# A new order and new bank numbers for the steps of a software-pipelined Trainium2 kernel

## The reference

```python
x = L0_attn_a_hidden_states                                  # (16, 256, 128)
x = x + _L0_attn_a_ref(_layernorm(x, axis=-1), ...)          # gated log-linear attention, 32 heads of 64
x = x + _L0_ffn_ref(_layernorm(x, axis=-1), ...)             # "layer 0"
x = x + _L0_attn_b_ref(_layernorm(x, axis=-1), ...)          # gated mix of 9 shifted copies
x = x + _L0_ffn_ref(_layernorm(x, axis=-1), ...)             # "layer 1", same weights
```

## Time and profile before

| | |
|---|---|
| time, three runs | 2206.03, 2209.48, 2211.31 us (median 2209.48) |
| the profiled execution | 2206.03 us, its span from first to last instruction 2204.2 us |
| mean granted TensorE clock | 0.963 of full speed |
| busy share of the span | PE 89%, PEld 68%, DVE 79%, ACT 67%, POOL 42% |
| chain that ended last | PE 66%, DVE 17%, ACT 6%, issue 5%, POOL 4%, DMA 1% |

### The profile page before, as it was taken

One profiled execution on the slowest core, in us unless ns is written; L12 is line 12 of the kernel. 1 busy time (PEld: TensorE's weight loads), 2 busy tenths in 40 slices (PEclk: granted clock), 3 DMA queues, 4 the chain that ended last, 5 costly groups with the idle time before them and its releaser, 6 DMA issues.

```text
span 2204.2 us, 48465 instructions
## 1 busy us (share of the span) xinstructions
PE 1965.1 (89%) x16928; PEld 1494.5 (68%) x16928; DVE 1738.6 (79%) x4399; ACT 1486.3 (67%) x3143; POOL 929.0 (42%) x1299
## 2 busy tenths in 40 slices
PE   4779888999999999999999999999999999996756
PEld 2556666686767677776767777676767777674534
DVE  6666787989888888889898888989888888754543
ACT  3646667868676777868686877868676877744323
POOL 5212362625444453635445453635445453523221
PEclk9889999999999999999999999999999999998868
DMA  5020221130312122130312222130212222121010
GB/s 155 7 56 11 50 57 50 36 60 21 60 44 57 52 57 53 33 60 22 57 48 57 52 57 53 33 61 21 58 48 57 52 54 53 34 53 46 13 46 6
DMA packets 202306, 104.59 MB, mean 47 GB/s; under 512 B 126664, under 2 KB 188240, under 8 KB 196944
## 3 DMA queue, kind: packets, MB, share of 16 engines
q1 hardware_dynamic: 202064, 101.48, 20.2%
HBM read 67.60 MB, written 33.55 MB: 46 GB/s over the span
## 4 chain that ended last, share of the span: by engine, by line
PE 66%; DVE 17%; ACT 6%; issue 5%; POOL 4%; DMA 1%; SPq 0%; DVEq 0%; POOLq 0%; ACTq 0%
PE psB L861 8%; PE psA L711 6%; PE psA L686 5%; PE psA L849 5%; PE psB L849 4%; PE psA L617 4%; PE psA L790 3%; DVE work L1201 3%; DVE nmax L1276 3%; PE psB L617 2%; PE psB L790 2%; PE psA L678 2%; PE psB L775 2%; PE psA L861 2%; ACT att L980 2%
## 5 line engine op out<-in xcount | busy, mean ns | idle before, releaser
L1228 DVE TENSOR_TENSOR att<-att,QK 128x1024 f32<-128x1024 f32 x192 | 267.6, 1427 | 19.1 <-ACT att L980 17.6
L1201 DVE SCALAR_TENSOR_TENSOR work<-psA,c_conv_w,work 128x254 f32<-128x254 f32 (+1 forms) x540 | 231.2, 472 | 23.8 <-ACT work L943 23.8
L1515 POOL TENSOR_TENSOR own<-X,ccoef 128x512 f32<-128x512 f32 x128 | 169.4, 1328 | 147.5 <-PE psA L686 68.9
L861 PE MATMUL psB<-c_w,hid 128*128 128x128 f32 x1664 | 221.7, 280 | 1.5 <-DVE hid L1349 0.7
L1412 POOL TENSOR_SCALAR var_eps<-lnmv 128x2 f32<-128x2 f32 x128 | 40.7, 318 | 430.9 <-DVE lnmv L1087 429.4
L861 PEld LDWEIGHTS psB<-c_w,hid 128*128 128x128 f32 x1664 | 211.2, 196 | 10.8 <-issue 1.5
L617 PE MATMUL psA<-xnT_a,c_w_in 128*128 128x256 f32 x640 | 189.3, 401 | 19.7 <-DVE hid L1201 11.3
L1276 DVE TENSOR_REDUCE nmax<-psB 128x2 f32<-128x512 f32 x256 | 168.6, 680 | 47.3 <-PE psB L752 47.3
L1357 DVE SCALAR_TENSOR_TENSOR ff<-psB,w_e,ff 128x128 f32<-128x128 f32 x416 | 126.5, 346 | 83.4 <-PE psB L861 81.4
L1026 ACT ACTIVATE pt<-psB 128x512 f32<-128x512 f32 x304 | 176.5, 633 | 11.7 <-PE psB L776 11.7
L1049 ACT ACTIVATE hid<-psB,c_b 128x256 f32<-128x256 f32 x233 | 105.5, 477 | 101.5 <-PE psB L849 99.9
...
## 6 DMA issues: line engine op xcount, KB each, us to landing
qk_scr<-qparts SPq DMA_DIRECT2D x128, 192.0 KB, 2.5
...
q_max<-qk_scr SPq DMA_DIRECT2D x256, 32.0 KB, 1.9
k_max<-qk_scr SPq DMA_DIRECT2D x256, 32.0 KB, 1.8
...
low<-lvl_scr SPq DMA_DIRECT2D x256, 1.5 KB
...
```

Source lines behind the costliest of these rows:

```text
L861: m = e.matmul(t[:, i * P:(i + 1) * P], hb[:, j, i * P:(i + 1) * P], w_2[:, 2 * k + j, :], start=(j == 0), stop=(j == 1))
L1201: m = e.scalar_tensor_tensor(out=cv[:, back:], in0=t[:, 0:T - back], scalar=conv_w[:, c, tap:tap + 1], in1=cv[:, back:], op0=ALU.mult, op1 ...
L1228: e.tensor_tensor(att[:, :, :], att[:, :, :], bc(QK[:, kq, :], 1, HG), ALU.mult).then_inc(att_done, 1)
L1515: e.tensor_tensor(own_b[k % 2][:, :].rearrange("p (h c) -> p h c", c=HD), X[:, tt, h0 * HD:(h0 + HG) * HD].rearrange("p (h c) -> p h c", c ...
```

## The change

`PERIOD` is replaced as a whole. It still holds the same 303 hops, each once; no instruction is added, taken out or resized by the text itself, and `order()`, `build()` and everything else stay. What is new is the order, the lags that belong to another cut of the turn, and most bank digits. The number of table loads follows from the order.

```diff
 PERIOD = """
-... zact0.6+1 xcopy0.4+1 zgate0.1+1@52 smax0.1+2@3576 zact0.1+1 silu0.6+1
-zgate0.3+1@04 rowmax0.0+2 silu0.7+1 zact0.3+1 mix1.1+3@14 tail1.4+4@5 rowmax0.1+2 coef0.0+1 mix1.2+3@1 mix1.3+3@7
-mix1.4+3@6 mix1.5+3@0 tail1.5+4@3 tail1.6+4 mix1.6+3@5 place0.0+1@7 relu1.0+4 mix1.7+3@2 mix1.8+3@3 taps0.8+1 lvl0.7+1
-tap0.8+1 rowmax0.2+2 own0.0+1 mix1.9+3@6 up1.0+4@05 conv0.8+1@01 mix1.10+3@5 zact0.7+1 zgate0.7+1@65 smax0.2+2@0732
-rowmax0.3+2 wexp0.0+1 weigh0.0+1@54 weigh0.1+1@10 xt0.6+1@7 weigh0.2+1@45 wexp0.1+1 wexp0.2+1 smax0.3+2@3216
-zgate0.4+1@40 mix1.11+3@3 xcopy0.6+1 zact0.4+1 prod0.0+1 ...
...
+... place0.0+1@1 ... xt0.4+1@0 zact0.6+1 zgate0.5+1@24 rowmax0.0+2
+smax0.0+2@0563 zgate0.6+1@72 zgate0.2+1@17 zact0.2+1 zact0.1+1 smax0.1+2@5126 zgate0.1+1@73 mix1.1+3@47 tail1.4+4@5
+rowmax0.1+2 coef0.0+1 mix1.2+3@3 mix1.3+3@2 mix1.4+3@3 tail1.5+4@4 tail1.6+4 up1.0+4@25 mix1.5+3@6 mix1.6+3@3
+up1.1+4@40 conv0.8+1@17 taps0.8+1 tap0.8+1 zgate0.7+1@63 own0.0+1 relu1.1+4 relu1.0+4 mix1.7+3@4 zact0.7+1 xt0.6+1@0
+mix1.8+3@2 smax0.2+2@1365 rowmax0.2+2 xcopy0.6+1 silu0.8+1 experts1.0+4@4 mix1.9+3@2 mix1.10+3@0 weigh0.0+1@40
+rowmax0.3+2 weigh0.2+1@12 wexp0.0+1 smax0.3+2@3765 wexp0.2+1 experts1.1+4@4 down1.0+4@3 v0.0+2@1 mix1.11+3@0 relu1.2+4
+up1.2+4@27 lvl0.6+1 weigh0.1+1@04 acc1.0+4 wexp0.1+1 down1.1+4@5 weigh0.3+1@63 wexp0.3+1 zgate0.4+1@70 prod0.0+1
+mix1.12+3 xt0.7+1@1 ... maxt0.0+2@3 ... gates0.1+0@6 xcopy0.7+1 ... xcopy0.5+1
...
```

More of the change, by code:

```diff
@@ L123 @@
 PERIOD = """
[L124 to L128, removed]
@@ L144 @@
-maxt0.0+2@7 xt0.7+1@5 gated0.0+1 fn1.0+3 xt0.5+1@0 gates0.1+0@6 xcopy0.5+1 acc1.1+4 up1.3+4@27 prod0.1+1 own0.1+1
-xcopy0.7+1 relu1.3+4 gates0.2+0@63 sum0.1+1@1 fn1.1+3@2 prod0.2+1 gated0.1+1 exps0.0+2 own0.2+1 es0.0+2@6304 own0.3+1
-q1.0+3@7 own0.4+1 sum0.2+1@2 gates0.3+0 weigh0.4+1@1674 ep0.0+2@0 wexp0.4+1 exps0.1+2 gated0.2+1 es0.1+2@3167
-ocopy0.0+2 down1.2+4@5 q1.1+3@4 gates0.4+0@3 ep0.1+2@1 es0.2+2@5634 ocopy0.1+2 acc1.2+4 up1.4+4@12 sum0.3+1@0
-weigh0.5+1@6715 prod0.3+1 prod0.4+1 gated0.3+1 ep0.2+2@4 es0.3+2@2630 gates0.5+0 exps0.2+2 sum0.4+1@7 weigh0.6+1@1432
@@ L149 @@
-ep0.3+2@6 sum0.5+1@0 own0.5+1 relu1.4+4 weigh0.7+1@4521 prod0.5+1 own0.6+1 wexp0.5+1 exps0.3+2 ocopy0.2+2 prod0.6+1
-wexp0.6+1 gated0.5+1 acc1.3+4 down1.3+4@6 tail0.0+2@45 ocopy0.3+2 prod0.7+1 wexp0.7+1 sum0.6+1@3 tail0.1+2@1
-sum0.7+1@0 gated0.6+1 gated0.4+1 gated0.7+1 own0.7+1 tail0.2+2@4 up1.5+4@51 down1.4+4@3 relu1.5+4 smax1.0+3@4751
-outp0.0+1@2 ssq0.0+1@6 gates0.6+0 smax1.1+3@4350 ssq0.1+1 acc1.4+4 ssq0.2+1 ssq0.3+1 smax1.2+3@1437 outp0.1+1
-smax1.3+3@4305 tail0.3+2
+weigh0.6+2@2610 gated0.4+2 exps0.3+3 tail0.0+3@53 sum0.5+2@2 ocopy0.2+3 load_x0.0+0 ocopy0.3+3 relu1.5+5 prod0.6+2
@@ new lines @@
+wexp0.6+2 tail0.1+3@7 weigh0.7+2@1463 v1.0+4@0 prod0.7+2 own0.7+2 acc1.4+5 tail0.2+3@5 down1.4+5@7 down1.5+5@4
+sum0.6+2@1 wexp0.7+2 acc1.5+5 smax1.0+4@0574 lvl0.0+1 sum0.7+2@6 smax1.1+4@1503 outp0.0+2@2 gated0.5+2 smax1.2+4@4560
+ssq0.0+2@3 lvl0.1+1 ssq0.1+2 gated0.6+2 rowmax1.0+4 gated0.7+2 ssq0.2+2 ssq0.3+2 smax1.3+4@1574 up1.6+5@60 rowmax1.1+4
+relu1.6+5 tail0.3+3 rowmax1.2+4 outp0.1+2 tail0.4+3@0 up1.7+5@74 rowmax1.3+4 maxt1.0+4@1 relu1.7+5 conv0.0+1@56
+lvl0.2+1 outp0.2+2 tap0.0+1 tail0.5+3@0 fn0.0+2 lvl0.3+1 down1.6+5@3 acc1.6+5 relu0.1+3 up0.1+3@24 taps0.0+1
@@ new lines @@
+es1.0+4@1032 exps1.0+4 up0.0+3@71 relu0.0+3 lvl0.4+1 exps1.1+4 tail0.6+3 ep1.0+4@0 es1.1+4@3514 acc1.7+5 down1.7+5@7
+conv0.1+1@26 tap0.1+1 ocopy1.0+4 experts0.0+3@3 ep1.1+4@5 experts1.2+5 es1.2+4@7134 exps1.2+4 fn0.1+2@0 taps0.1+1
+experts0.1+3@7 ocopy1.1+4 ocopy1.2+4 ep1.2+4@1 q0.0+2@4 experts1.3+5 es1.3+4@0257 exps1.3+4 gates0.0+0 down0.0+3@1
+conv0.2+1@20 tap0.2+1 up0.2+3@36 down0.1+3@5 relu0.2+3 up0.3+3@41 silu0.0+1 silu0.1+1 tap0.3+1 conv0.3+1@67 acc0.0+3
+taps0.2+1 bcp0.0+1 down0.2+3@3 relu0.3+3 xt0.0+1@5 q0.1+2@0 up0.4+3@24 acc0.1+3 acc0.2+3 relu0.4+3 silu0.2+1
@@ new lines @@
+rowmax0.3+2 weigh0.2+1@12 wexp0.0+1 smax0.3+2@3765 wexp0.2+1 experts1.1+4@4 down1.0+4@3 v0.0+2@1 mix1.11+3@0 relu1.2+4
+up1.2+4@27 lvl0.6+1 weigh0.1+1@04 acc1.0+4 wexp0.1+1 down1.1+4@5 weigh0.3+1@63 wexp0.3+1 zgate0.4+1@70 prod0.0+1
+mix1.12+3 xt0.7+1@1 lvl0.7+1 sum0.0+1@2 zact0.4+1 maxt0.0+2@3 acc1.1+4 gates0.1+0@6 xcopy0.7+1 prod0.1+1 xcopy0.5+1
+xt0.5+1@4 fn1.0+3 prod0.2+1 up1.3+4@03 relu1.3+4 own0.1+1 gated0.0+1 gates0.2+0@57 down1.2+4@1 own0.2+1 exps0.0+2
+acc1.2+4 es0.0+2@3627 sum0.1+1@4 fn1.1+3@0 prod0.3+1 sum0.2+1@5 gates0.3+0 own0.3+1 weigh0.4+1@2716 gated0.1+1
@@ L154 @@
+wexp0.4+1 ep0.0+2@3 q1.0+3@0 ocopy0.0+2 up1.4+4@72 own0.4+1 es0.1+2@4105 gated0.2+1 own0.5+1 exps0.1+2 sum0.3+1@6
+gates0.4+0@4 relu1.4+4 gated0.3+1 ep0.1+2@1 ocopy0.1+2 q1.1+3@5 prod0.4+1 es0.2+2@4236 gates0.5+0 exps0.2+2
+down1.3+4@0 acc1.3+4 prod0.5+1 gates0.6+0 weigh0.5+1@1745 own0.6+1 ep0.2+2@3 es0.3+2@2671 sum0.4+1@4 ep0.3+2@7
+wexp0.5+1 up1.5+4@53
 """
```

17 lines of the change are left out of this document (6 added, 11 removed).

## The result

| | before | after |
|---|---|---|
| time | 2210.39 us median of four (2206.03 to 2212.87) | 2223.94 us median of four (2221.42 to 2225.14) |
| ratio | | 1.0062, 95% interval 1.0043 to 1.0081 |
| span of the profiled execution | 2204.2 us | 2222.1 us |
| mean granted TensorE clock | 0.963 | 0.961 |

What follows compares the result with a forecast made beforehand. DVE was taken to bound 23.7 us of each 124.2 us turn, PE the rest. Terms -2.1 + 0.6 + 0.3 = -1.2 us per turn, times 13 = 15.6 us, gave 2193 us, 0.7% faster; range 2160 to 2225.

Steps and rivals of the forecast that it cites:

- The sign of being wrong: Turns of 124 us or longer though the DVE stretch got shorter, or ramp and tail moved by more than 8 us.
- For these 23.7 us the kernel is bound by DVE, for the other 100 by PE: Steady turn: DVE sets the pace from `tail1.2`'s readout to the last `rowmax0.3`, PE elsewhere; 5.2 us of PE idle there.
- The instructions are the same, so a turn has the same work for PE, DVE, POOL and DMA: Whole steady turn: reordering leaves these engines' work unchanged, so only four places in the turn were costed.
- Place 4: POOL and all other banks: `gates0.6` ahead of `own0.6` and new bank digits cost nothing, within 1 us per turn either side.
- Place 1: The stretch that DVE bounds: PE gets 1.44 us more work, DVE 0.68 us less; 2.1 us per turn won.
- rival B: DVE-bound stretch: the waits only move to the next bank, no change, 2209 us; chance 0.14.
- Place 2: ScalarE from `wexp0.0` to `gates0.2`: table loads rise from 98 to 126, 2.57 us per turn, 0.6 us on the path.
- The disputed price: Cost of a table switch on ScalarE: 1.29 us in the trace, against 2.66 us with the skill's drain.
- Rival A: ScalarE's queue from `mix` to `exps0.2` takes over as the bound: slower, 2225 us at full load price; chance 0.24.
- Place 3: Layer 1 maxima: `es1.0` has less cover for the DMA of `maxT` and waits 0.3 us more per turn.
- Ramp and tail: Start and end outside the steady turns: nothing gained or lost, 8 us to either side.
- TensorE's clock at its upper level throughout: Twelve steady windows: clock taken as 1.00, or 2.4 GHz, in all of them.

Runs made afterwards that it cites:

- experiments 1 and 3: Kernel after, `gates0.6` moved back behind `tail0.2`: 2231.09 us; kernel after, GpSimd's large `gates0.6` instructions made to wait for VectorE's five: 2244.1 us, with 98 table loads 2241.84.
- Experiment 5: Kernel after with `gates0.6` moved behind `gated0.7`, into GpSimd's idle gap: 2203.01 us, ratio 0.9985 to the kernel before.
- experiment 1: Kernel before with `gates0.6` moved directly behind `prod0.5`, as in the new order: 2258.38 us; the reverse move in the kernel after: 2231.09 us.
- experiment 6: Kernel before with `place0.0` moved ahead of `tail1.2`: 2213.74 us; kernel before with `zgate0.6` moved behind `smax0.0`: 2206.90 us.
- experiment 2: Kernel after with 98 table loads: 2224.25 us (`zgate0.4`, `zact0.4` moved), 2226.09 us (order unchanged); kernel before with 126 loads, nothing moved: 2267.64 us.
- experiment 5's second kernel: Kernel after with `gates0.6` moved behind `gated0.7` and 98 table loads instead of 126: 2206.22 us, ratio 0.9995 to the kernel before.
- experiment 7: Kernel before, `prod0.2` moved ahead of `gates0.2`: 2225.81 us; kernel after with `gates0.6` behind `gated0.7`, `prod0.2` moved later in three variants: 2213.65, 2217.48, 2216.38 us.

## Why the prediction was wrong, point by point

The measured ratio puts the kernel after at 2223.9 us, inside the range given and on the other side of no change. The likeliest case was forecast as 0.7% faster. The sign of being wrong that the prediction names came true: turns over 124 us although stretch A did get shorter.

- **"For these 23.7 us the kernel is bound by DVE, for the other 100 by PE": this step failed.** It was read off idle time of PE, which says where another engine has overtaken PE, and not how near it is elsewhere. In stretch C, DVE had been busy for 24.33 of 26.5 us and PE for 26.33, so there were 2.2 us between "PE bounds" and "DVE bounds". The new order used them up.
- **"The instructions are the same, so a turn has the same work for PE, DVE, POOL and DMA": failed with it.** The count is the same, the work isn't: DVE's busy time rose by 50.4 us in eleven turns, 4.6 us per turn. Three terms make up three quarters of it: L1178 and L1182 21.6 us (11 x 2 x 0.98), L1176 and L1180 9.4 us, L1091 of `xn_a` 7.3 us, each while something large on GpSimd runs beside it. The longer durations are not the cost by themselves, though: experiments 1 and 3 take most of them away, and the undisturbed turns stay at 125.6 to 126.2 us, as the hop then holds up DVE's readouts or GpSimd's `own0.6` in another way.
- **Place 4, "I cost it at nothing": the mis-sized term.** The cover that I named for `gates0.6` was that GpSimd is idle for half of a turn. It is, but not in that half. Experiment 5 gives 17 us back by this one hop, in the turn (1.4 us at an equal clock) and in the ramp; experiment 1 shows the same move costing 3.6 us per turn of the old order, 2.5 of them in undisturbed turns. The bound of 1 us per turn for all of place 4 was drawn from bank waits and left out GpSimd's queue altogether.
- **Place 1 was right in size, and the two parts of it that were tried won nothing by themselves.** -2.1 us were forecast, -2.5 measured in stretch A; L752's wait for L1276, 1.13 us in the earlier trace rows, is 0.3 us at the longest after. But experiment 6 shows that neither of two parts that I counted shortens the turn of the old order: not DVE's 0.68 us, and not the 0.87 us of cover. The rest of it (`up1.1`, `experts1.0` and `experts1.1` inside the stretch, `up1.0` further ahead) was not tried alone. In the old order the waits move (rival B's mechanism, at this place). In the new order PE's gain of 2.5 us ran into stretches B and C, which give 4.5 back. That the gain in A and the loss in B are one and the same thing is only argued: PE reaches B sooner and DVE doesn't.
- **Place 2: the count was right, the price was not.** 126 loads came, as forecast. The 0.6 us per turn came out as 0: experiment 2 takes all 28 loads away and gains nothing, and neither does experiment 5's second kernel. The same pair in the old order costs 4.5 us per turn: 2.6 in undisturbed turns, the high end of 2.57, and the rest with the clock that went down. The disputed price is settled as far as rows go: the next exp starts 1.30 us after the load starts, as in the earlier trace rows. ScalarE after:

```profile
1153.30 1.28 ACT L903 ACT_TABLE_LOAD   x1
1154.60 0.60 ACT L980 ACTIVATE att<-psA 128x512 f32<-128x512 f32 x1
```

  By the Trainium skill (ScalarE: Activation LUTs, What ACT_TABLE_LOAD costs) there would be 1.38 us of drain on top; this trace has no room for it. Rival A, ScalarE as the bound, gave nearly the measured time, and by a mechanism that the runs exclude.
- **Place 3 had the wrong sign, and a small size.** The wait of the earlier trace rows for the DMA of `maxT` stands in one turn of eleven before and in none after, not in every turn. `es1.0` itself got 0.20 us shorter (1.07 to 0.87 us), not 0.3 longer.
- **Ramp and tail, "nothing, 8 us to either side":** the ramp gave 13.0 us and the tail took 5.6; together -7.4, inside.
- **"TensorE's clock at its upper level throughout" was not so.** Two of the windows between the two of the earlier trace rows have 0.99 and 0.97, and take 124.9 and 125.7 us. The prediction has no term for the clock; before against after it is worth 0.2 us of the 2.0 per turn, but in some experiments about 2.
- **Stretch B stays half open.** It costs 1.5 us per turn. Experiment 2 excludes the loads, experiment 7 shows that `prod0.2`'s place costs the old order 1.5 us and can't be undone in the new one. Which of the many other differences sets it was not found.
